# A message sum on one Trainium2 core: three exact bf16 parts for the values, bf16 one-hots for the rows, and part of both made on the scalar engine

## What is computed

```
diff = edge_vectors[:, None, :] - mu[None, :, :]
gauss = jnp.exp(-0.5 * jnp.sum(diff * diff / (EPS + sigma[None] ** 2), axis=-1))
xj = x[src] @ g
msg = jnp.sum(xj.reshape(e, k, cout) * gauss[:, :, None], axis=1)
summed = jax.ops.segment_sum(msg, dst, num_segments=n)
```

## Time and profile before

| | |
|---|---|
| median of 3 runs | 7194.07 us (7187.43 to 7205.15) |
| the profiled execution | 7204.02 us, span of the core 7201.8 us |
| busy: PE, PEld | 4555.3 us (63%), 3352.2 us (47%) |
| busy: DVE, ACT, POOL | 4068.6 us (56%), 1735.2 us (24%), 4447.1 us (62%) |
| mean granted TensorE clock | 0.868 of full speed |
| DMA | mean 61 GB/s |

### The profile page before, as it was taken

How to read it: one execution, slowest core, us unless ns; L and a number is a source line. 1 busy time by engine, 2 the same in 40 slices (tenths; PEclk the granted TensorE clock), 3 DMA queues, 4 the chain that set the end, 5 groups by cost and what they waited for, 6 DMA issues and landing times. The chain is left out here.

```text
span 7201.8 us, 95745 instructions
## 1 busy us (share of the span) xinstructions
PE 4555.3 (63%) x31067; PEld 3352.2 (47%) x31067; DVE 4068.6 (56%) x9109; ACT 1735.2 (24%) x3107; POOL 4447.1 (62%) x4319
## 2 busy tenths in 40 slices
PE   5444442866478888886655569999992455444433
PEld 4444442655356666664543435555551333333322
DVE  7555553679666666665432227777763544444443
ACT  1111111557544444443320000000001222222211
POOL 2777776110177777776525247777755777777764
PEclk9999999989889999998877789999996777777766
DMA  4222221133322222226858461111111111111384
GB/s 74 73 80 73 73 75 37 32 104 159 133 52 53 53 54 53 53 53 44 36 66 236 172 216 38 37 37 37 37 33 21 19 19 18 19 18 18 18 15 14
DMA packets 388370, 441.44 MB, mean 61 GB/s; under 512 B 241123, under 2 KB 312240, under 8 KB 387901
## 3 DMA queue, kind: packets, MB, share of 16 engines
q0 software_dynamic: 137696, 130.26, 17.0%
q1 hardware_dynamic: 194073, 289.05, 12.7%
q10 hardware_dynamic: 56528, 21.19, 1.3%
HBM read 358.39 MB, written 82.34 MB: 61 GB/s over the span
## 5 line engine op out<-in xcount | busy, mean ns | idle before, releaser
L951 POOL DMA_INDIRECT at_far<-att_table,at_rec x1184 | 1223.7, 1033 | 879.8 <-DMA at_rec<-rec_r 399.3
L1524 POOL DMA_INDIRECT p_far<-table,p_rec x1184 | 1244.9, 1051 | 482.9 <-issue 360.2
L2299 PE MATMUL g_l_ps_sum<-g_l_row,g_l_of 128*128 128x392 f32 x3224 | 1063.7, 493 | 19.3 <-DVE g_l_of L2250 19.3
L534 POOL DMA_INDIRECT rec_r<-so_r_rec,so_r_place x806 | 835.6, 1037 | 245.5 <-issue 245.5
L2221 POOL DMA_INDIRECT g_l_got<-table,g_l_index x806 | 814.8, 1011 | 245.5 <-issue 227.8
L2299 PEld LDWEIGHTS g_l_ps_sum<-g_l_row,g_l_of 128*128 128x128 f32 x3224 | 613.9, 190 | 469.6 <-DVE g_l_of L2250 20.4
L1422 PE MATMUL at_bank<-p_spread,p_basis 64*125 64x256 f32 x4736 | 628.0, 418 | 107.9 <-ACT p_outer L1477 107.9
L1422 PE MATMUL p_ps_outer<-p_spread,p_basis 128*125 128x256 f32 x2368 | 604.3, 422 | 60.8 <-DVE p_spread L1367 52.7
L489 PE MATMUL so_r_look<-so_r_table,so_r_lo_t 128*128 128x26 f32 x1612 | 425.0, 434 | 311.1 <-DVE so_r_table L433 311.1
L1422 PEld LDWEIGHTS at_bank<-p_spread,p_basis 64*125 64x125 f32 x4736 | 519.2, 199 | 205.0 <-ACT p_outer L1477 146.4
L1477 ACT COPY p_outer<-at_bank 125x512 f32<-125x512 f32 x1184 | 587.1, 758 | 36.0 <-PE at_bank L1422 33.0
(11 more groups left out here) (472 smaller groups left out, 6363.3 us busy)
## 6 DMA issues: line engine op xcount, KB each, us to landing
adjacent<-ad_by_chunk SPq DMA_DIRECT2D x74, 800.0 KB, 3.3
so_r_row<-pad_src SPq DMA_DIRECT2D x62, 832.0 KB, 6.2
g_l_counts<-adjacent SPq DMA_DIRECT2D x60, 800.0 KB, 7.2
g_l1d_counts<-adjacent SPq DMA_DIRECT2D x59, 800.0 KB, 7.2
so_r_low<-pad_lo_src SPq DMA_DIRECT2D x62, 416.0 KB, 4.6
at_far<-att_table,at_rec POOLq DMA_INDIRECT x1184
p_far<-table,p_rec POOLq DMA_INDIRECT x1184
rec_r<-so_r_rec,so_r_place POOLq DMA_INDIRECT x806, 2.1
```

The costliest lines, as they stand in the source:

```text
L534: pool.indirect_dma_start(out=o.rec[:, :], out_offset=bass.IndirectOffsetOnAxis(ap=place[b][:, j:j + 1], axis=0), in_=rec[b][:, j, :], in_ ...
L951: pool.indirect_dma_start(out=far[b][:, t, :], out_offset=None, in_=g.att_table[:, :], in_offset=bass.IndirectOffsetOnAxis(ap=rec[b][:, t, ...
L1524: pool.indirect_dma_start(out=sl.far[b][:, t, :], out_offset=None, in_=table[:, :], in_offset=bass.IndirectOffsetOnAxis(ap=sl.rec[b][:, t, ...
L2299: last = nc.tensor.matmul(ps_sum[k][:], of4[b][:, j, :, :].rearrange("p k f -> p (k f)"), row1[b][:, j, k * COLS:(k + 1) * COLS], start=Fa ...
```

## The change

1. **Values.** After `of4` is made (now one buffer, f32), it is cut into three bf16 matrices whose sum is exactly the f32 value: part 0 is `of4` rounded to bf16, part 1 the rest rounded, part 2 what is left then. The two roundings are casts on the scalar engine (lines 2350 and 2353, 128x1664), the two subtractions are on the vector engine (lines 2273 and 2280, three pieces each). Each needs the one before, so the data goes from vector to scalar engine and back twice in a step (`cut`, `rest`, `cut`, `parted`).
2. **One-hots.** `row1` is bf16. The vector engine makes 9 of 13 of them (line 2238), the scalar engine 4 (lines 2340 and 2342: |row - iota|, then max(0, 1 - that), each 784 wide, the second waiting for the first).
3. **Matmuls.** For each tile three parts times two banks, in bf16, one instruction each: 78 a step in place of 52 (line 2322). TensorE waits for `parted` and `hots` in place of `ready`.
4. **Order.** The vector engine now mixes first and makes the one-hots behind that: four behind the mix, five behind the first subtraction. The wait for `summed` and for its own `parted` stands ahead of the mix. The indices of the step after the next are written right behind the mix, as before. The pieces of 13 tiles are 4, 4 and 5 in place of 5, 4 and 4. GpSimd's code is unchanged.

```diff
-        of4 = [sb(f"of4{b}", [P, HB, 4, F]) for b in two]
-        row1 = [sb(f"row1{b}", [P, HB, TALL]) for b in two]
+        of4 = sb("of4", [P, HB, 4, F])
+        part = [[sb(f"part{b}{k}", [P, HB, 4, F], BF16) for k in range(3)] for b in two]
+        row1 = [sb(f"row1{b}", [P, HB, TALL], BF16) for b in two]
+        apart = sb("apart", [P, TALL])
+        by_dve = HB - 4
...
+                pieces = ((0, 4), (4, 8), (8, HB))
...
+                def one(step, b, turn, first=False, last_pair=False):
+                    if not first:
+                        dve.wait_ge(summed, step - 1)
+                        dve.wait_ge(parted, step)
+                    mix(step, b, turn)
+                    if not last_pair:
+                        index_of(step + 2, b)
+                    one_hots(step, b, range(by_dve // 2))
+                    dve.wait_ge(cut, step * 2 + 1)
+                    for at, end in pieces:
+                        here = nc.vector.tensor_sub(of4[:, at:end], of4[:, at:end], part[b][0][:, at:end])
+                    here.then_inc(rest, 1)
+                    one_hots(step, b, range(by_dve // 2, by_dve))
+                    ch.wait()
+                    dve.wait_ge(cut, step * 2 + 2)
+                    for at, end in pieces:
+                        here = nc.vector.tensor_sub(part[b][2][:, at:end], of4[:, at:end], part[b][1][:, at:end])
+                    here.then_inc(parted, 1)
...
-                        pe.wait_ge(ready, i * 2 + (b + 1))
+                        pe.wait_ge(parted, i * 2 + (b + 1))
+                        pe.wait_ge(hots, i * 8 + (4 * b + 4))
                         for j in range(HB):
-                            for k in two:
-                                last = nc.tensor.matmul(ps_sum[k][:], of4[b][:, j, :, :].rearrange("p k f -> p (k f)"),
-                                                        row1[b][:, j, k * COLS:(k + 1) * COLS], start=False, stop=False)
+                            for of in part[b]:
+                                for k in two:
+                                    last = nc.tensor.matmul(ps_sum[k][:], of[:, j, :, :].rearrange("p k f -> p (k f)"),
+                                                            row1[b][:, j, k * COLS:(k + 1) * COLS], start=False, stop=False)
...
             @block.scalar
             def _(act):
+                def one_hots(step, b, js):
+                    for j in js:
+                        act.wait_ge(hots, step * 4 + (j - by_dve))
+                        nc.scalar.activation(apart[:], iota[:], ACT.Abs, bias=g.edge_row[:, bass.ds(step * HB + j, 1)], scale=-1.0).then_inc(aparts, 1)
+                        act.wait_ge(aparts, step * 4 + (j - by_dve + 1))
+                        nc.scalar.activation(row1[b][:, j, :], apart[:], ACT.Relu, bias=g.ones[:, 0:1], scale=-1.0).then_inc(hots, 1)
+                def one(step, b, first=False):
+                    if not first:
+                        act.wait_ge(summed, step - 1)
+                    one_hots(step, b, range(by_dve, by_dve + 2))
+                    act.wait_ge(ready, step + 1)
+                    nc.scalar.copy(part[b][0][:], of4[:]).then_inc(cut, 1)
+                    one_hots(step, b, range(by_dve + 2, HB))
+                    act.wait_ge(rest, step + 1)
+                    nc.scalar.copy(part[b][1][:], of4[:]).then_inc(cut, 1)
```

More of the change, by code:

```diff
@@ L2207, in stage_messages @@
         gathered = [rows_sem(nc, f"{name}_gathered{b}") for b in two]
+        cut, rest, parted, hots, aparts = (sem(n) for n in ("cut", "rest", "parted", "hots", "aparts"))
         iotas, steps, indexed, mixes, ready, summed, all_in, copied, turned, out, stored, taken = (
@@ L2247, in mix @@
                     ch.step(nc.vector.tensor_add(mixed[:], mixed[:], rows3[:, :, 2, :]))
-                    for at, end in ((0, 5), (5, 9), (9, HB)):
+                    for at, end in pieces:
                         b4, here = [P, end - at, 4, F], bass.ds(step * HB + at, end - at)
-                        last = nc.vector.tensor_mul(of4[b][:, at:end, :, :], mixed[:, at:end, :].unsqueeze(2).to_broadcast(b4),
+                        last = nc.vector.tensor_mul(of4[:, at:end, :, :], mixed[:, at:end, :].unsqueeze(2).to_broadcast(b4),
                                                     g.edge_of4[:, here, :].unsqueeze(3).to_broadcast(b4))
                     last.then_inc(ready, 1)
+                def one(step, b, turn, first=False, last_pair=False):
[7 more added lines that the diff above has]
+                    dve.wait_ge(cut, step * 2 + 1)
+                    for at, end in pieces:
+                        here = nc.vector.tensor_sub(of4[:, at:end], of4[:, at:end], part[b][0][:, at:end])
[3 more added lines that the diff above has]
+                    dve.wait_ge(cut, step * 2 + 2)
+                    for at, end in pieces:
+                        here = nc.vector.tensor_sub(part[b][2][:, at:end], of4[:, at:end], part[b][1][:, at:end])
+                    here.then_inc(parted, 1)
                 for b in two:
@@ L2261, in _ @@
                 dve.sem_inc(mixes, 1)
[L2262 to L2265, removed]
+                one(0, 0, 0, first=True)
+                dve.wait_ge(parted, 1)
+                one(1, 1, 0, first=True)
                 with dve.Fori(1, half - 1) as i:
@@ L2268, in _ @@
                     for b in two:
[L2269 to L2274, removed]
+                        one(i * 2 + b, b, i)
                 ch.restart()
                 for b in two:
-                    dve.wait_ge(summed, STEPS - 3 + b)
-                    one_hots(STEPS - 2 + b, b)
-                    mix(STEPS - 2 + b, b, half - 1)
+                    one(STEPS - 2 + b, b, half - 1, last_pair=True)
                 full, left = divmod(WIDE, P)
@@ L2312, in _, with one_hots @@
             def _(act):
+                def one_hots(step, b, js):
+                    for j in js:
+                        act.wait_ge(hots, step * 4 + (j - by_dve))
[11 more added lines that the diff above has]
+                    nc.scalar.copy(part[b][1][:], of4[:]).then_inc(cut, 1)
+                act.wait_ge(mixes, 1)
+                for b in two:
+                    one(b, b, first=True)
+                with act.Fori(1, half) as i:
+                    for b in two:
+                        one(i * 2 + b, b)
                 for k in two:
```

3 lines of the change are left out of this document (removed).

## The result

The changed kernel takes 7229.0 us in the median of 20 runs, the kernel before 7205.7 in the 20 runs beside them: a ratio of 1.0032 (95% interval 1.0025 to 1.004). It is slower by 23 us, on the forecast side, at half of the forecast size (+45). The kernel before had a median of 7194 in the three runs shown ahead of the prediction and 7206 in all 20. The start of the forecast was thus 12 us too low and its difference 22 us too large, and the two errors partly cancel: that the time itself (7229 against 7238) is off by 9 us only is luck. In the profiled executions the spans are 7233.4 and 7201.8; of these 31.6 us, 4.3 lie ahead of the stage (the first gather starts at 4301.1 in place of 4296.8).

The account below looks back on a forecast made before the run. PE (17.15 us a step) and POOL (17.10) were both taken as full. POOL's step growing to 17.77 over 62 steps gives +41.5 us, the tail +3, together +45: 7238 us, range 7170 to 7305.

Parts of the forecast that it names:

- Both engines full before, POOL left as the limit after: Gather stage: PE at 17.15 us a step and POOL at 17.10 both full; after the change POOL sets the end.
- the second rival: POOL's stretch stays about what it was, one of three additions absent: step 16.7 to 17.4, 7194 us; chance 0.24.
- POOL's step of 17.77: POOL's new step: 13 undisturbed gathers at 16.24 us plus 1.53 of stretch, up from 17.10.
- The mix, priced at 0.56: Stretch of gathers that start during the vector engine's mix: 0.56 us a step, kept as before (0.25 + 0.31).
- The subtractions, priced at 0.47: Stretch of gathers from six two-input subtraction instructions on the vector engine, 4.06 us of work: 0.47 us a step more.
- The entries into the one-hots: Stretch of gathers as a one-hot run begins: two entries a step instead of one, 0.25 us each, 0.5 together.
- The vector chain of 14.9: Vector engine's work a step once its gathers have landed, mix through second subtraction: 14.4 to 15.1 us, taken as 14.9.
- PE's 12.9: 78 bf16 matmuls a step at 0.165 us each: 12.9 us in place of 17.15.
- the third rival: PE's clock drops as PE idles some 4.8 us a step: at 0.71, 18.2 us a step, +71 us; chance 0.04.
- The scalar engine: Eight activations and two casts a step, semaphores included: 11.2 us, fitting beside 16.24 with nobody waiting for its total.
- The one-hots priced like f32 ones: Vector engine's one-hots with bf16 output keep the fast form; if lost, 1.01 us each and a chain of 19.
- The first rival: Gathers fall in step with the new order: step under 16.7, at 16.5 a time of 7160 us; chance 0.15.

Follow-up runs that it names:

- experiments 3 to 5 and 7: Experiment 3, experiment 4, experiment 7, and one more: the kernel before with 10 of 13 gathers a step, 7196.0 us, ratio 0.9996.
- experiment 3: Changed kernel with the first bf16 part alone: no subtractions, no second cast, 26 matmuls a step in place of 78; 7173.9 us, ratio 0.9963.
- experiment 7: Kernel before with both matrices (of4, row1) in bf16 and nothing else, messages rounded to bf16; 7166.7 us, ratio 0.9962.
- experiment 2: Changed kernel with each of the two subtractions as one instruction of 1664 elements in place of three pieces; 7326.6 us, ratio 1.0175.
- experiment 4: Changed kernel with 10 of 13 gathers a step, three tiles of each buffer holding zeros; 7056.1 us, ratio 0.9801.
- the first kernel of experiment 9: Experiment 7 with three unused 512-element products of two SBUF tiles added behind the mix; run again, 7178.9 us, ratio 0.998.

## Why the prediction was right, and where it was off

- **Both engines full before, POOL left as the limit after.** Right, and shown by experiments 3 to 5 and 7 and by the unchanged 245.5 us of idle in the changed kernel.
- **How narrowly.** The measured step of 17.46 lies 0.06 us above 17.4, where the second rival ends (the stretch stays about what it was, since one of the additions is absent). One addition was indeed nearly absent, as the next point says. The difference of 23 us is 2 us over the 21.6 that the prediction took for no change. The mechanism of the forecast held; that it came out on this side of that line is in part luck.
- **POOL's step of 17.77.** Right in kind, too long; measured 17.46. By the terms of the sum, in the mean of all 62 steps: 16.24 is right (the shortest 13 gathers took 16.23). The mix, priced at 0.56, stretches by 0.37 + 0.19 = 0.56, though at other moments. The subtractions, priced at 0.47, cost 0.42 + 0.12 = 0.54 (0.55 by experiment 3). **The entries into the one-hots were mis-sized**: 0.5 for two, measured 0.12. The one entry in the kernel before cost 0.34 in the step that the prediction read and 0.27 in the mean; there PE's end decided when the one-hots began. In experiment 7, with the same order and no wait for PE, it costs nothing (0.00 in the mean), so that the price was one of the moment at which the run of one-hots began and could not be carried over. The entries are 0.38 us a step too high, 24 us, and the subtractions 0.07 too low, 4 us: together the difference between +41.5 and +22.2.
- **The vector chain of 14.9** from landing to `parted`: 4860.66 to 4875.13 is 14.5, within the range given (14.4 to 15.1). The second cast never kept it waiting in the loop (0.3 us once, in the last step).
- **PE's 12.9.** At full clock it is right: two matmuls are 0.166 us apart, and the quickest bursts of 78 take 13.1 us. But the median burst takes 14.8, because the clock is low at or near its start: 0.57 of full speed from 4857 to 4861, 1.00 from 4861 to 4872. The difference is hidden in the loop and shows once, in the tail, where the last burst takes 14.8 us in place of 13.1. Without that the tail would have grown by 2.5 us, near the 3 forecast, in place of 4.2. For the same reason PE is busy for 83% of the stage and not for the 73% that the prediction named as a sign. In that the third rival was partly real, and its reason for not deciding (the pause has room for a slow start) held.
- **The scalar engine** at 11.2: eight activations of 0.947 and two casts of 1.57 are 10.7, without waits.
- **The one-hots priced like f32 ones.** Right: with bf16 output the one-hots kept the fast form, 0.666 in the mean against 0.694 before.
- **The first rival** (the gathers fall in step) was half right: the second entry costs 0.02 us a step and the second subtraction 0.12, a quarter of the first one's 0.42. This is the part which the forecast lacked.

## What to carry to other kernels

Before relieving the engine that looks like the limit, add busy and fixed idle time of the next one: an engine whose idle time is the same 0.3 us ahead of each of its 806 instructions is full, though its busy share says 77%. Where GpSimd issues indirect DMAs all the time, long vector instructions cost it time whoever waits for whom; cut them short (a vector instruction of 0.6 us held a gather up by up to 0.50 us, one of 1.9 us by up to 1.27), and count an added pass over data by that too. Here PE's relief, priced at 263 us (its busy time fell by 158), was worth nothing in the end, and two passes of 2 us a step on an engine with room cost 34.

## What the runs showed of the hardware

- An indirect DMA of 128 rows costs POOL 0.944 + 0.305 us, and 13 in a row never took under 16.22. If a vector instruction with two SBUF inputs or a one-hot (one f32 input in SBUF) is under way at its start, it is longer by what that instruction has still to go, less some 0.13 us: 295 gathers of the changed kernel, 302 of experiment 2. A gather that starts in the first 0.06 us of such an instruction is often not held (64 of 73 in the first kernel of experiment 9). With one of two inputs in PSUM there is no such wait (0.94 us beside a product with 1.08 to go).
- Gathers and vector instructions fall in step: one wait puts the next starts on later edges where the lengths fit (two one-hots and a gather, two 512-wide products and a gather). Stretch is thus a matter of a few fixed places in a step and not a share of time; 1.53 us a step was forecast and 1.23 measured.
- TensorE's granted clock fell to its lower level in or just after most pauses of the changed kernel and came back within the same burst. After 50 of its 61 pauses (1.4 to 4.5 us long) 8 to 18 matmuls at or near the start of the burst are 0.33 us apart and the rest 0.166; after the other 11 all are 0.166 apart. In experiment 4, where the pauses ahead of a burst were 1.7 us in the mean (92.0 us in 54 waits), the clock stayed at 1.00.
